# One load of 18 tile numbers per body, another order of PSUM banks, and a slot ring refilled in three parts, in a graph-network kernel of 49-tile passes

## The chip, the cores and the metric

The program runs on one core of one Trainium2 chip. The metric is the device time of one execution in microseconds (us), lower is better. A run of the program before takes 8250.26 us (median of 3).

## The reference

The work is a two-block graph transformer on 6250 nodes with 256 features and 100,000 edges sorted by destination. The part that the change touches is the sum over edges:

```python
def _rgcn_layer(X, W, root, bias, gamma, beta, src, dst, etype, inv_deg):
    h = jnp.einsum('ni,rio->rno', X, W)              # table of 4 x 6250 rows
    msg = h[etype, src] * inv_deg[:, None]
    agg = jax.ops.segment_sum(msg, dst, num_segments=X.shape[0])
    out = agg + X @ root + bias
    ...                                              # layer norm, elu, + X
for l in range(4): X = _rgcn_layer(X, ...)           # block 0
...
agg = segment_sum(all_h[src, rel], dst)              # block 1, once, 8 relations
```

Beside block 0 a linear-attention mixer on the same rows is computed (keys and values summed over all rows, then attention rows with a layer norm, then a feed-forward with a layer norm), beside block 1 the keys of a second mixer. Feed-forward stages follow both.

## The kernel before, in words

**Five passes over the edges.** The edges are cut into steps of 128 edges, and 17 steps (`SLOTS`) make a body; 49 bodies (`NT`) make a pass. There are four passes for block 0 (called passes 0 to 3 here) and one for block 1 (pass 4). In a body the engines do this, each in a hardware loop (`Fori`) of its own, joined by semaphores alone:

- POOL (`EdgeSum.gpsimd`, L530) issues one indirect DMA for each step, which gathers 128 message rows into slot s of `msg`.
- PE (`EdgeSum.tensor`, L579) multiplies the step's one-hot matrix `hot` (edge to row of the tile) by the messages into a PSUM bank.
- DVE (`EdgeSum.vector`, L559) adds the bank to the sum of the step's tile, whose number it reads from a register. It reads the numbers of the next 9 steps with `load_tiles` (L81, a register load from SBUF) ahead of step 0, and those of the other 8 ahead of step 9. A third load (`ranked_tile`, L88) of one word stands at the start of a body in passes 0 to 3.
- DVE makes 9 of the 17 one-hot matrices (L539), ACT the other 8 (`scalar_hots`: L508, L511, L520).
- ACT (`ring`, L497 and L498) copies the row numbers and edge data of the next body into a small ring, in two halves: steps 0 to 8 once PE has done them, then 9 to 16. POOL waits for that ring (`slots_copied`) before it gathers.

**Banks.** Step s uses bank 4 + s mod 4, so PE may be four steps ahead of DVE.

**What runs between the steps.** After step s each engine calls the hook `after(s)` of two other pieces. `Post` finishes one tile of the layer (norm, elu, new state: L624 to L649 on DVE after steps 0 to 8; transposes L672 and products L678, L684 on PE after steps 11 to 16; copies L694, L696, L701 on ACT), and SP stores the tile's two halves of the next table (L706). The mixer piece is `Keys0` in pass 0 (PE L785 and L791, ACT L801 to L803, DVE L811 and L814), `Attend` in pass 1 (PE L874 and L937, ACT L862, L950, L951, DVE L961) and `Feed` in pass 2 (PE L867, L874 and L1054, ACT L862, L1065, L1069). Pass 3 has only `Post` without the products, pass 4 only the keys of the second mixer. In these pieces the order on each engine is written out by hand; a wait blocks all that stands behind it on its engine.

## Time and profile before

| | |
|---|---|
| runs shown | 8244.22, 8250.26, 8263.54 us |
| profiled execution, its own time | 8245.88 us |
| its span in the trace | 8244.1 us |
| mean granted TensorE clock | 0.823 |
| busy: PE, DVE, POOL, ACT | 5874.8, 4269.0, 4208.5, 2931.9 us |
| passes 0, 1, 2 (first to last gather) | 571.9 to 1796.1, 1829.0 to 3072.8, 3108.4 to 4251.3 us |
| passes 3, 4 | 4280.0 to 5322.7, 6334.0 to 7373.9 us |

Busy times are sums of instruction durations on one engine, so they overlap. Idle time in a row (in square brackets) is that of the engine just before the instruction, with the one whose end released it; "issue" is idle time for which the profile shows no releaser. A matmul row with `x2` is one fp32 product in two passes.

### The profile page before, as it was taken

The numbers are of one execution on the slowest core, as the hardware profiler recorded it, in microseconds if no ns is written. First come the engines' busy times: TensorE is split into PE (matmuls) and PEld (weight loads), VectorE is DVE, ScalarE is ACT, GpSimd is POOL, SyncE is SP. The second block draws the span as 40 slices with busy tenths as digits, with TensorE's granted clock in tenths as the row PEclk, the third lists the DMA queues.
The fourth block names the chain that finished last, engine by engine and source line by source line (L and its number), as shares of the span: only waits on it lengthen the run. The fifth ranks groups of instructions, "written<-read, shape, count | busy, mean of one in ns | idle before, by whom it ended". The sixth has DMA issues, their size and how long they took to land. (4 is left out here: it accounts for less than half of the span.)

```text
span 8244.1 us, 110504 instructions
## 1 busy us (share of the span) xinstructions
PE 5874.8 (71%) x17886; PEld 3559.1 (43%) x17886; DVE 4269.0 (52%) x14582; ACT 2931.9 (36%) x8048; POOL 4208.5 (51%) x4288
## 2 busy tenths in 40 slices
PE   0487777767777776777768888788498777763398
PEld 0244444444444444554443333355344444443265
DVE  7215555546666665666656666522434666652412
ACT  0133333333444445666653333222022444431132
POOL 0016666656666656777667777600002777753211
PEclk9998888888888888889985556589599888877699
DMA  1444333334444434444443333300044333330000
GB/s 56 145 132 118 112 116 114 113 115 121 124 124 123 123 117 134 135 135 135 132 151 105 104 105 105 99 0 0 19 142 132 105 105 105 105 87 1 13 14 18
DMA packets 478956, 811.01 MB, mean 98 GB/s; under 512 B 88600, under 2 KB 343148, under 8 KB 478657
## 3 DMA queue, kind: packets, MB, share of 16 engines
q0 software_dynamic: 200480, 548.02, 23.2%
q1 hardware_dynamic: 278430, 262.51, 9.9%
q8 instruction: 13, 0.21, 0.0%
q14 instruction: 33, 0.27, 0.0%
HBM read 614.04 MB, written 196.16 MB: 98 GB/s over the span
## 5 line engine op out<-in xcount | busy, mean ns | idle before, releaser
L530 POOL DMA_INDIRECT gnn_msg<-tables,gnn_row_ring x4165 | 3985.8, 957 | 2183.9 <-issue 1585.2
L579 PE MATMUL bank<-gnn_msg,gnn_hot 128*128 128x256 f32 x8330 | 3143.3, 494 | 781.0 <-DVE sums L559 506.8
L559 DVE TENSOR_TENSOR sums<-sums,bank 128x256 f32 x4165 | 1746.0, 419 | 2060.0 <-PE bank L579 1360.7
L579 PEld LDWEIGHTS bank<-gnn_msg,gnn_hot 128*128 128x128 f32 x8330 | 1748.2, 237 | 2130.3 <-DVE sums L559 1424.8
L133 POOL TENSOR_TENSOR ve<-mv,eps 128x7 f32<-128x7 f32 x35 | 7.1, 204 | 1348.6 <-DVE mv L127 1200.3
L520 ACT ACTIVATE gnn_hot<-gnn_away,gnn_meta_ring 128x128 f32<-128x128 f32 x1568 | 645.8, 482 | 47.3 <-ACT gnn_meta_ring L511 0.8
L684 PE MATMUL bank<-gnn_w,residual 128*128 128x512 f32 x1176 | 620.1, 610 | 33.7 <-DVE sums L652 33.7
L508 ACT ACTIVATE gnn_away<-iota,gnn_meta_ring 128x128 f32<-128x128 f32 x1960 | 625.5, 391 | 24.0 <-ACT gnn_meta_ring L498 0.2
L539 DVE TENSOR_SCALAR gnn_hot<-iota,gnn_meta_ring 128x128 f32<-128x128 f32 x1764 | 629.1, 357 | 0.5 <-ACT gnn_meta_ring L498 0.5
L497 ACT COPY gnn_row_ring<-row 128x9 int32 (+1 forms) x490 | 94.9, 194 | 1070.3 <-PE bank L579 1058.5
L1760 PE MATMUL bank<-tables_w,sums 128*128 128x512 f32 x784 | 340.1, 596 | 6.4 <-ACTq L117 6.4
L701 ACT COPY residual<-bank 128x512 f32<-128x512 f32 x294 | 172.1, 585 | 284.0 <-PE bank L684 284.0
L684 PEld LDWEIGHTS bank<-gnn_w,residual 128*128 128x128 f32 x1176 | 219.9, 197 | 116.1 <-DVE sums L652 83.3
L658 ACT ACTIVATE gnn_own<-gnn_own 128x256 f32<-128x256 f32 x196 | 81.7, 417 | 442.2 <-DVE gnn_own L638 442.2
L1219 PE MATMUL bank<-gnn_w,gnn_hot 128*128 128x512 f32 (+1 forms) x588 | 221.0, 534 | 19.7 <-ACTq L1284 19.7
L1760 PEld LDWEIGHTS bank<-tables_w,sums 128*128 128x128 f32 x784 | 149.4, 191 | 193.2 <-issue 193.2
L678 PE MATMUL bank<-gnn_w,residual 128*128 128x256 f32 x588 | 222.3, 518 | 1.6 <-ACT residual L696 1.4
L874 PE MATMUL bank<-residual 128*128 128x128 f32 x784 | 155.5, 363 | 66.9 <-ACT residual L1065 64.5
L862 ACT ACTIVATE residual<-residual,gnn_own 128x256 f32<-128x256 f32 x98 | 58.8, 600 | 402.0 <-DVE residual L849 402.0
L696 ACT COPY residual<-bank 128x256 f32<-128x256 f32 x147 | 54.7, 372 | 395.3 <-PE bank L672 395.0
L874 PEld LDWEIGHTS bank<-residual 128*128 128x128 f32 x784 | 145.1, 269 | 107.2 <-ACT residual L1065 94.0
L1773 DVE COPY sums<-bank 128x512 f32<-128x512 f32 x98 | 67.7, 691 | 230.8 <-PE bank L1760 226.7
(390 smaller groups left out, 6866.1 us busy)
## 6 DMA issues: line engine op xcount, KB each, us to landing
tables<-residual SPq DMA_DIRECT2D x294, 256.0 KB
gnn_msg<-tables,gnn_row_ring POOLq DMA_INDIRECT x4165, 2.8
tables<-sums SPq DMA_DIRECT2D x98, 512.0 KB, 2.9
tables<-gnn_msg SPq DMA_DIRECT2D x98, 256.0 KB, 2.1
residual<-first_norm_columns SPq DMA_DIRECT2D x98, 128.0 KB, 2.4
first_norm<-state SPq DMA_DIRECT2D x1, 6272.0 KB, 21.4
first_rows<-residual SPq DMA_DIRECT2D x1, 6272.0 KB, 39.2
residual<-first_norm SPq DMA_DIRECT2D x49, 128.0 KB, 3.1
```

The lines of the kernel that those rows point to most:

```text
L508: self.nc.scalar.activation(self.away[:, k, :], self.c.iota[:], ACT.Abs, bias=m[:, u, 0:1], scale=-1.0)\
L520: ins = self.nc.scalar.activation(to, self.away[:, k, :], ACT.Relu, bias=m[:, u, 1:2], scale=m[:, u, 2:3])
L530: self.nc.gpsimd.indirect_dma_start(out=self.msg[:, s0 + u, :], out_offset=None, in_=table, in_offset=bass.IndirectOffsetOnAxis(ap=self.ro ...
L539: ins = self.nc.vector.tensor_scalar(to, self.c.iota[:], m[:, 0:1], m[:, 1:2], ALU.is_equal, ALU.mult)
L559: self.nc.vector.tensor_tensor(at, at, self.sums(s), ALU.add).then_inc(self.added, 1)
L579: self.nc.tensor.matmul(self.sums(s), self.hot[:, s, :], self.msg[:, s, :], start=True, stop=True).then_inc(self.summed, 1)
L678: ins = t.matmul(c.bank[1][:, 0:D], self.xt[:, h, :], self.w[:, h, REL0 * D:], start=(h == 0), stop=(h == KH - 1))
L684: ins = t.matmul(c.bank[3 - 2 * j][:], self.xt[:, h, :], self.w[:, h, j * 512:(j + 1) * 512], start=(h == 0), stop=(h == KH - 1))
L701: self.nc.scalar.copy(self.outs[:, j, :], self.c.bank[3 - 2 * j][:]).then_inc(self.s_out, 1)
L874: ins = self.nc.tensor.matmul(self.c.bank[0][:, m * P:(m + 1) * P], weights[:, h, m * P:(m + 1) * P], self.xt[:, h, :], start=(h == 0), st ...
L1219: ins = nc.tensor.matmul(c.bank[b][:, 0:width], xt[:, h, k * P:(k + 1) * P], w[:, h, j * 512:j * 512 + width], start=(h == 0), stop=(h == ...
L1760: ins = nc.tensor.matmul(c.bank[b][:], xt[:, h, k * P:(k + 1) * P], w[:, h, j * 512:(j + 1) * 512], start=(h == 0), stop=(h == KH - 1))
```

## The change

1. **Tile numbers.** `body_row` holds 18 words for each body: its 17 tile numbers and, behind them, the number of the tile that `Post` finishes. DVE loads all 18 once at the start of a body (`body_tiles`), in place of `load_tiles` twice and `ranked_tile` once. The row begins at the same SBUF address as before; a body's words now begin at word 18 i, where they began at words 17 i and 17 i + 9.
2. **Banks.** Steps 0 to 7 use banks 4 to 7 twice, steps 8 to 16 use banks 4, 5, 6 three times. Step 0 of a body follows step 14 on its bank, where it followed step 16.
3. **Three parts.** The ring is refilled in parts of 6, 6 and 5 steps. ACT makes 3 one-hot matrices in each (9 in all), DVE 3, 3 and 2 (8). On ACT part 0's refill moves ahead of the exponential, and part 0's one-hot matrices ahead of the copies of `Post.turned`.
4. **Mixer.** SP fetches the mixer rows of body i + 1 between the two table stores of body i, where it fetched them at the start of body i + 1. On PE the mixer's first products move from after step 5 to after step 3 (`Keys0`, `Attend`), in `Feed` from after steps 3, 6, 10 to after 2, 5, 9. On DVE `Attend`'s L961 moves from after step 9 to after step 6, and its L964 from 6 to 9.

```diff
-HALVES = ((0, 9), (9, 8))
+PARTS = ((0, 6), (6, 6), (12, 5))
-SUM_SLOTS = 4
+SUM_BANKS = (4, 5, 6, 7, 4, 5, 6, 7, 4, 5, 6, 4, 5, 6, 4, 5, 6)
...
-def load_tiles(eng, c, first, n):
-    regs = c.regs[str(eng.engine)][:n]
-    eng.reg_load(regs, c.tile_row[0:1, ds(first, n)])
+def body_tiles(eng, c, i):
+    regs = c.regs[str(eng.engine)]
+    eng.reg_load(regs, c.body_row[0:1, ds(i * (SLOTS + 1), SLOTS + 1)])
     return [eng.snap(r, min_val=0, max_val=NT - 1) for r in regs]
...
-DVE_HOTS = (5, 4)
-ACT_HOTS = 4
-NEXT_HOTS = (((), (), (0,), (), (1,), (), (2,), (), (3,)),
-             ((), (), (0,), (1,), (), (2,), (3,), (4,)))
+DVE_HOTS = (3, 3, 2)
+ACT_HOTS = 3
+NEXT_HOTS = (((), (), (0,), (), (1,), ()),
+             ((), (), (0,), (), (1,), (2,)),
+             ((), (), (0,), (1,), (2,)))
...
     def vector(self, dve, tiles, n, after, last=False):
-        for h, (s0, w) in enumerate(HALVES):
-            tiles = load_tiles(dve, self.c, i * SLOTS + s0, w)
-            for u, t in enumerate(tiles):
+        for h, (s0, w) in enumerate(PARTS):
+            for u in range(w):
                 s = s0 + u
+                t = tiles[s]
...
     def tensor(self, pe, n, after):
-            back = s - SUM_SLOTS + 1 if s >= SUM_SLOTS else max(k for k in range(SLOTS) if k % SUM_SLOTS == s) + 1 - SLOTS
-            pe.wait_ge(self.added, n * SLOTS + (SLOTS + back))
+            before = max(k for k in range(s - SLOTS, s) if SUM_BANKS[k] == SUM_BANKS[s])
+            pe.wait_ge(self.added, n * SLOTS + (SLOTS + before + 1))
...
 (SP, passes 0 to 2)
-                    with sp.Fori(1, NT) as i:
-                        work.sync(sp, i, True, True)
-                        post.sync(sp, i + l * NT, ranked_tile(sp, c, i - 1), c.tabs[(l + 1) % 2])
+                    with sp.Fori(1, NT - 1) as i:
+                        t = ranked_tile(sp, c, i - 1)
+                        work.store(sp, i, True, True)
+                        post.sync(sp, i + l * NT, t, c.tabs[(l + 1) % 2], 0)
+                        work.load(sp, i + 1)
+                        post.sync(sp, i + l * NT, t, c.tabs[(l + 1) % 2], 1)
...
 (ACT, passes 0 to 2)
                         work.scalar(act, i, True, True)
+                        edges.ring(act, i + 1, n + 1, 0)
                         post.exponential(act, n)
-                        edges.ring(act, i + 1, n + 1, 0)
+                        edges.scalar_hots(act, n + 1, 0)
                         post.turned(act, n, t)
-                        edges.scalar_hots(act, n + 1, 0)
+                        edges.ring(act, i + 1, n + 1, 1)
+                        edges.scalar_hots(act, n + 1, 1)
                         post.way_out(act, n, 0)
-                        edges.ring(act, i + 1, n + 1, 1)
+                        edges.ring(act, i + 1, n + 1, 2)
                         post.way_out(act, n, 1)
-                        edges.scalar_hots(act, n + 1, 1)
+                        edges.scalar_hots(act, n + 1, 2)
```

How this stands on the engines is shown at three places. Line numbers of the changed kernel are its own (L559 is L565 there, L520 is L525).

DVE at the start of the loop of pass 0, before: one word of `order` is loaded, then nine of `tile_row`, and then comes step 0's add.

```order
L1374 ISA
L88 TENSOR_LOAD order
L89 ISA
L81 TENSOR_LOAD tile_row
L82 ISA
L556 REGISTER_ALU
L557 REGISTER_ALU [waits steps_summed]
L559 ISA [waits steps_added]
L559 TENSOR_TENSOR sums<-sums,bank 128x256
```

Further down in the same body DVE had, between the last piece after step 8 and step 9's add:

```order
L649 SCALAR_TENSOR_TENSOR residual<-gnn_own,state 128x256
L81 ISA
L81 TENSOR_LOAD tile_row
L82 ISA
L559 ISA [waits steps_added,steps_summed]
L559 TENSOR_TENSOR sums<-sums,bank 128x256
```

The changed kernel has one load at the start, and none between steps 8 and 9:

```order
L1394 ISA
L81 TENSOR_LOAD body_row
L82 ISA x2
L562 REGISTER_ALU
L563 REGISTER_ALU [waits steps_summed]
L565 ISA [waits steps_added]
L565 TENSOR_TENSOR sums<-sums,bank 128x256
```

Three loads with 1 + 9 + 8 words have become one load with 18.

ACT in the body of pass 0, from the mixer's results to the copies of the new state, before (`post_turned` is signalled by PE's transposes L672):

```order
L803 COPY residual<-bank 128x2x128
L658 ACTIVATE gnn_own<-gnn_own 128x256 [waits gnn0_post_normal]
L661 ACTIVATE gnn_own<-gnn_own 128x256 [waits gnn0_post_negative_part]
L494 ISA
L497 ISA [waits steps_summed]
L497 COPY gnn_row_ring<-row 128x9
L498 ISA
L498 COPY gnn_meta_ring<-meta 128x9x2
L694 ISA [waits gnn0_post_state_made]
L694 COPY state<-residual 128x256
L696 COPY residual<-bank 128x256 [waits gnn0_post_turned]
```

The same stretch of the changed kernel:

```order
L503 COPY gnn_meta_ring<-meta 128x6x2
L664 ACTIVATE gnn_own<-gnn_own 128x256 [waits gnn0_post_normal]
L667 ACTIVATE gnn_own<-gnn_own 128x256 [waits gnn0_post_negative_part]
L509 ISA
L513 ACTIVATE gnn_away<-iota,gnn_meta_ring 128x128 [waits slots_copied]
L513 ACTIVATE gnn_away<-iota,gnn_meta_ring 128x128 x2
L516 ACTIVATE gnn_meta_ring<-gnn_meta_ring 128x6
L519 ISA
L525 ACTIVATE gnn_hot<-gnn_away,gnn_meta_ring 128x128 [waits distances_made]
L525 ACTIVATE gnn_hot<-gnn_away,gnn_meta_ring 128x128 x2
L700 ISA [waits gnn0_post_state_made]
L700 COPY state<-residual 128x256
```

The ring's copies now stand ahead of the two activations of the exponential, and seven activations for part 0's one-hot matrices stand between the exponential and the two copies.

SP in the loop of pass 0 in the changed kernel (L740 is the mixer's columns, L711 a table store):

```order
L711 ISA [waits gnn0_post_evicted]
L711 DMA tables_1<-residual 128x2x256
L739 REGISTER_ALU
L740 ISA [waits gnn0_keys_products]
L740 DMA residual<-first_norm_columns 128x256
L710 REGISTER_ALU
L711 ISA [waits gnn0_post_evicted]
L711 DMA tables_1<-residual 128x2x256
```

The columns stand between the two stores; before, they stood behind both and the loop's branch.

## Rows read from the trace of the kernel before

**Rows 1.** Windows, passes 0 to 4: length, busy PE, PEld, DVE, ACT, POOL, then PEclk.

```profile
700.00:1700.00 1000.00, 744.25 (x2203) 454.41 (x2203) 545.65 (x1868) 396.21 (x1221) 641.99 (x672) 0.84 0.39 114
1900.00:2900.00 1000.00, 729.41 (x2345) 470.02 (x2346) 618.80 (x2149) 401.07 (x1210) 642.25 (x666) 0.85 0.42 123
3200.00:4200.00 1000.00, 736.92 (x2640) 497.58 (x2640) 649.65 (x2260) 611.43 (x1494) 704.46 (x727) 0.89 0.46 135
4400.00:5200.00 800.00, 699.40 (x1277) 303.02 (x1276) 486.54 (x1649) 279.27 (x904) 605.54 (x638) 0.58 0.36 105
6500.00:7300.00 800.00, 569.05 (x1875) 360.81 (x1874) 493.74 (x2078) 329.02 (x1127) 604.96 (x641) 0.83 0.36 105
```

**Rows 2.** Waits in 700 to 1700 us (pass 0): total us, times, longest.

```profile
POOL gnn_msg L530 <- ACT gnn_meta_ring L498: 169.0, 69, 3.3
DVE sums L559 <- issue: 163.7, 70, 3.6
PEld bank L791 <- DVE residual L811: 162.2, 40, 4.5
```

**Rows 3.** Timeline of DVE, pass 0: adds of step 9, 0, 9, 0.

```profile
965.26 0.42 DVE L559 TENSOR_TENSOR sums<-sums,bank 128x256 f32 x1 [0.46 <-issue]
...
978.91 0.42 DVE L559 TENSOR_TENSOR sums<-sums,bank 128x256 f32 x1 [1.71 <-PE bank L579]
...
1016.55 0.42 DVE L559 TENSOR_TENSOR sums<-sums,bank 128x256 f32 x1 [1.69 <-issue]
...
1032.03 0.42 DVE L559 TENSOR_TENSOR sums<-sums,bank 128x256 f32 x1 [3.60 <-issue]
```

**Rows 4.** Timeline of DVE, step 0's adds: one in pass 3, two in pass 4.

```profile
4606.21 0.42 DVE L559 TENSOR_TENSOR sums<-sums,bank 128x256 f32 x1 [3.00 <-PE bank L579]
...
6511.34 0.42 DVE L559 TENSOR_TENSOR sums<-sums,bank 128x256 f32 x1 [1.19 <-PE bank L579]
...
6533.80 0.42 DVE L559 TENSOR_TENSOR sums<-sums,bank 128x256 f32 x1 [2.42 <-PE bank L579]
```

**Rows 5.** Timeline of PE in pass 0, and of ACT's one-hot matrices.

```profile
966.27 1.20 PE L791 MATMUL bank<-residual 128*128 128x129 f32 x4 [2.88 <-DVE residual L814]
...
1002.23 1.27 ACT L508 ACTIVATE gnn_away<-iota,gnn_meta_ring 128x128 f32<-128x128 f32 x4
...
1003.73 1.65 ACT L520 ACTIVATE gnn_hot<-gnn_away,gnn_meta_ring 128x128 f32<-128x128 f32 x4
```

**Rows 6.** Windows of 1 us in pass 0; PEclk is the third number from the end.

```profile
967.00:968.00 1.00, 1.00 (x5) 0.83 (x4) 0.00 (x0) 0.00 (x0) 0.83 (x1) 0.50 0.37 98
973.00:974.00 1.00, 1.00 (x5) 0.70 (x4) 0.25 (x1) 0.00 (x0) 0.70 (x2) 1.00 0.29 74
```

**Rows 7.** Timeline of one body of pass 1, from step 0's add.

```profile
2326.05 0.42 DVE L559 TENSOR_TENSOR sums<-sums,bank 128x256 f32 x1 [3.69 <-issue]
...
2333.93 0.42 ACT L661 ACTIVATE gnn_own<-gnn_own 128x256 f32<-128x256 f32 x1
...
2337.11 0.74 PE L937 MATMUL bank<-residual 128*128 128x132 f32 x4 [2.75 <-DVE residual L961]
...
2339.78 1.68 PE L678 MATMUL bank<-gnn_w,residual 128*128 128x256 f32 x4
```

**Rows 8.** Timeline of pass 2: end of a body, then the next body.

```profile
3604.36 0.30 PEld L684 LDWEIGHTS bank<-gnn_w,residual 128*128 128x128 f32 x2 [1.34 <-DVE sums L652]
...
3610.15 0.42 DVE L559 TENSOR_TENSOR sums<-sums,bank 128x256 f32 x1 [3.40 <-issue]
...
3611.83 0.66 PE L867 MATMUL bank<-ident,residual 128*128 128x128 f32 x2 [3.30 <-DMA residual<-mixer_rows]
...
3618.46 0.62 ACT L1069 ACTIVATE residual<-bank,residual 128x128 f32<-128x128 f32 x2 [0.86 <-PE bank L874]
...
3621.24 0.42 DVE L641 SCALAR_TENSOR_TENSOR gnn_own<-gnn_own 128x256 f32<-128x256 f32 x1 [1.39 <-ACT gnn_own L661]
...
3623.60 0.51 PEld L678 LDWEIGHTS bank<-gnn_w,residual 128*128 128x128 f32 x3 [0.35 <-ACT residual L696]
```

More of the change, by code:

```diff
@@ L779, in after @@
         def after(s):
-            if s == 5 and first:
+            if s == 3 and first:
                 pe.wait_ge(self.s_xt, i * 16 + 16)
@@ L927, in after @@
         def after(s):
-            if s == 5 and first:
+            if s == 3 and first:
                 pe.wait_ge(self.s_xt, i * 16 + 16)
@@ L1041, in after @@
         def after(s):
-            if s == 3 and first:
+            if s == 2 and first:
                 pe.wait_ge(self.s_dma, i * 16 + 16)
@@ L1973, in _ @@
                 gate(act, c)
-                for h in range(2):
+                for h in range(NPART):
                     edges.ring(act, 0, n0, h)
```

150 lines of the change are left out of this document (81 added, 69 removed).

## The prediction

> **What bounds the kernel now.** I read the windows over the five passes first. POOL issues 17 gathers for each body, so its count gives the time of a body: 17 x 1000 / 672 = 25.3 us in pass 0, 17 x 1000 / 666 = 25.5 in pass 1, 23.4 in pass 2, 21.3 in pass 3 and 21.2 in pass 4 [rows 1]. In passes 3 and 4 each gather follows the last after 800 / 640 = 1.25 us. POOL never rests there, so 21.25 us is the floor of a body as long as there are 17 gathers in it, and passes 3 and 4 stand on it. Passes 0 to 2 lie 4.1, 4.3 and 2.1 us above it. The change does not touch the gathers, so it can win (4.1 + 4.3 + 2.1) x 47 = 490 us at most. (I count 47 full bodies in a pass of 49; the first and last run without their neighbours.)
>
> In pass 0 POOL waits for the ring 69 times in 1000 us, 169 us together, but in that list no PE wait for a message stands among the long ones. POOL's waits follow from something else. The list names it: DVE stands idle 163.7 us in 70 waits for nothing the profile knows ("issue"), and PE's L791 waits 162.2 us in 40 bodies for DVE [rows 2]. The reader should see that PE and DVE take turns. At the start of a body PE runs its four steps ahead and then needs DVE's step 0; in the middle L791 needs DVE's L814 after step 9; from there to step 16 DVE follows PE. A stall of DVE ahead of step 0 or step 9 is therefore paid in full.
>
> Both stalls are register loads. Ahead of step 9 DVE is idle 1.69 us, or 0.46 in every fourth body; ahead of step 0 it is idle 3.60, or 1.71 in every fourth [rows 3]. The fast ones are the bodies in which the load begins at a word number that is a multiple of four (17 i or 17 i + 9); the other three remainders are alike. Four bodies hold 3 x 1.69 + 0.46 and 3 x 3.60 + 1.71, which is 1.38 + 3.13 = 4.5 us of stall a body.
>
> **The change, part by part.**
>
> *The loads.* I estimate a price for one word. Eight words cost 1.69 - 0.46 = 1.23 us more when they begin off a multiple of four, and nine words 2.42 - 1.19 = 1.23 in pass 4 [rows 3, 4]. If an unaligned load goes word by word and an aligned one by groups of four with single words left over, that is 8 against 2 reads and 9 against 3: six more both times, 0.205 us each, and 8 x 0.205 = 1.64 is the whole unaligned gap. The one-word load is the difference of pass 3 and pass 4, which has none: 3.00 - 2.42 = 0.58 [rows 4]. What is left at the start of a body is 1.19 - 3 x 0.205 = 0.57 for branch and rest. In pass 0 the unaligned start has 0.6 us more than in pass 3 (3.60 against 3.00); SP and ACT load words then too, so I keep it as a collision.
>
> Now 18 words begin at 18 i: a multiple of four in even bodies only. Even: 4 groups and 2 words, 0.57 + 6 x 0.205 = 1.8 us. Odd: 18 reads, 0.57 + 3.69 + 0.6 = 4.9 us. Mean 3.35, and nothing before step 9. Bounds: if 18 words cost 1.8 always, 1.8; if they never go by fours, 0.57 + 18 x 0.205 = 4.3; if the collision also grows with the words, 5.5. I take the middle, since both kinds of body are seen.
>
> The Trainium skill speaks against this part: "Runtime: NRT & Kernel Launch", Instruction fetch mechanics, gives about 200 ns for each register even in bulk. The unaligned rows agree with it, the aligned ones do not. By that rule 18 words before and 18 after cost the same 3.6 us, and only the fixed parts of two loads would be saved.
>
> *Pass 0.* Without its loads a body is 25.3 - 4.5 = 20.8 us. Added: 3.35, which gives 24.15. L785 moves ahead of step 4, into the time in which PE waits for DVE; that PE idle shrinks and costs nothing elsewhere. Its columns are fetched between the stores, which is sooner by one store and the branch. DVE makes one one-hot fewer by step 9 (-0.3), but with none after step 6 it meets the exponential 0.3 sooner and waits for it. ACT now makes three one-hots before the new state's copies: 1.27 + 1.65 for four plus 0.2 for the scaling is 3.15, so 2.42 for three [rows 5]. In pass 0 L672 comes only after L791, and ACT is free by then: hidden, with about 1.4 us to spare; without that cover it would add 1. One more term is PE's clock. After 2.88 us of idle PE starts L791 [rows 5], and the granted clock is 0.50 (1.2 GHz) at 967 us and 1.00 (2.4 GHz) again at 973 [rows 6]. PE's idle falls to about 2.3 us. Whether the clock still drops I can't tell from a row; full recovery would save about 2 us a body, none saves 0. I take 0.7, as the 2.88 of the nearest row still led to a drop. Body: 23.4, a gain of 1.9.
>
> *Pass 1.* The same stalls are there [rows 7]: 25.5 - 4.5 + 3.35 = 24.35. Here L937 waits 2.75 us for L961, which stood after step 9 and now stands after step 6. PE goes on until it needs the new state. ACT sets the next point: L661 ends 8.3 us after step 0's add (2326.05 to 2334.35), the one-hots take 2.42, the two copies 0.8, so L678 starts at 11.6 where it started at 13.7, 0.5 of which is the aligned load already counted. That is 1.6 earlier. PE's idle is now cut in small pieces, for which I take 0.6 of clock. Body: 22.2, a gain of 3.3.
>
> *Pass 2.* Here the middle load hides: DVE waits 1.39 for L661 before step 8 anyway, and PE waits 1.34 for L652 later on [rows 8]. ACT is the path: the norm, the copy, L1069 (which waits 0.86 for PE's L874), the exponential, then L694 and L696, then L678. The ring's copies ahead of the exponential add 0.3, the one-hots add 2.42 less the 1.4 that ACT idled there. On the other side PE no longer waits 3.30 for the mixer rows, so its clock should stay up in L874, which gives back the 0.86. From step 0's add (3610.15) L678 started at 13.45; now 11.1 + 0.3 - 0.86 + 2.42 + 0.8 = 13.75. That is 0.3 late. L684 waited 1.34 for L652, which now comes sooner; I count 0.7 of it, since DVE has its own instructions to do between step 9 and L652. The start costs 3.35 instead of some 3.0 (3.40 in the row, less the aligned quarter). The body is 23.4 + 0.3 - 0.7 + 0.35 = 23.3, a gain of 0.1; if none of the 1.34 comes back it is 24.0, if all does 22.7.
>
> *Passes 3 and 4.* The start of an odd body grows from 3.0 to about 4.3, but the load in the middle is gone, and POOL is the bound. POOL needs PE's step 16 only 12 gathers (15 us) after its own. Cost and gain nothing. The third ring wait, the new banks (step 11 now needs step 8's add instead of step 7's, in a stretch in which DVE waits for PE) and the two small copies in the preparation are hidden or below 1 us.
>
> *Sum.* (1.9 + 3.3 + 0.1) x 47 = 249 us. The profiled execution took 8245.9, which gives 7997. The median of the runs is 4 us higher; I say 7998.
>
> **Rivals.**
>
> (a) The clock recovers and the load is as I think: pass 0 goes to 22.1, pass 1 to its floor 21.3, pass 2 to 22.8. Another 2.7 x 47 = 127 us: 7870. For it: PE will be idle for less time at a stretch than ahead of the row in which the clock had fallen; against it, by little. Chance 0.15.
>
> (b) The load of 18 is cheap in all bodies (1.8): 21.85, 21.3 and 21.75, a gain of 9.3 x 47 = 437: 7809. For it speaks only that 8 and 9 words pay the same penalty, which a fixed penalty would explain too. Chance 0.12.
>
> (c) The load never goes by fours, 4.3 a body: 24.35, 23.15, 24.25, a gain of (0.95 + 2.35 - 0.85) x 47 = 115: 8131. This is the rule of the skill named above as a mechanism of this kernel; the aligned rows speak against it. Chance 0.13.
>
> (d) As (c), and ACT's new order eats what the clock and L961 would give: 25.0, 25.2, 24.1, together zero: about 8246. Chance 0.05.
>
> (e) Slower: the load costs 5.5 in every body, because a longer load meets SP's and ACT's own loads more often. The place is the start of the bodies of passes 0 to 2, where 4.5 is paid now. With pass 1 held at 21.0 + 5.5 it gives 25.6, 26.5 and 25.4, or (0.3 + 1.0 + 2.0) x 47 = 155 us more: 8401. It decides from about 4.9 us a load, if pass 1 gains nothing else. Only the 0.6 of collision speaks for it. Chance 0.08.
>
> **How the numbers follow.** My forecast has 0.47. The range 7860 to 8135 holds it with (a) and (c) and leaves out (b) and (e); the forecast's own range is 7930 to 8060. A measurement of this kernel can tell about 0.2% (16 us) from no change. Faster: 0.47 + 0.15 + 0.12 + 0.13 = 0.87; same 0.05; slower 0.08.
>
> **What the profile after would show.** No DVE idle before step 9; before step 0 an idle that alternates between about 1.8 and 4.9 us. Gathers per 1000 us: 726 in pass 0, 766 in pass 1, 730 in pass 2, and 1.25 us apart in passes 3 and 4 as before. In pass 1 L937 without a wait for DVE and L678 some 11.6 us after step 0's add; in pass 2 ACT's L696 late. I am wrong if the start of a body costs much more or less than 3.35 on average, if PE's clock behaves otherwise, or if passes 3 or 4 leave the floor.

## The result and the profile after

The changed kernel takes 8075.3 us (median of 4 runs, 8071.81 to 8077.64), the kernel before 8256.88 us in the runs beside it (4 runs, 8244.22 to 8263.54). The ratio is 0.9779, 95% interval 0.9765 to 0.9794. It is faster by 182 us where the prediction said 249, and 8075 lies 15 us outside the forecast's own range of 7930 to 8060, inside the wide one of 7860 to 8135. The profiled execution took 8071.81 us, its span is 8070.0 us, and its mean granted clock 0.81 (before 0.823).

Windows over passes 0 to 3 after the change (length, busy PE, PEld, DVE, ACT, POOL, PEclk):

```profile
700.00:1700.00 1000.00, 788.92 (x2337) 459.37 (x2338) 564.23 (x1927) 468.03 (x1499) 675.16 (x709) 0.85 0.41 120
1850.00:2850.00 1000.00, 820.63 (x2740) 508.30 (x2740) 711.01 (x2478) 517.02 (x1652) 741.77 (x770) 0.86 0.49 143
3050.00:4050.00 1000.00, 729.27 (x2511) 492.88 (x2512) 622.12 (x2104) 622.00 (x1623) 663.37 (x686) 0.84 0.43 127
4250.00:5050.00 800.00, 678.85 (x1273) 290.63 (x1272) 477.70 (x1614) 321.41 (x1082) 606.13 (x637) 0.61 0.36 104
```

Against [rows 1], pass 0 goes from 672 to 709 gathers (726 forecast), pass 1 from 666 to 770 (766 forecast), and pass 2 falls from 727 to 686 (730 forecast). Pass 2 has become slower. Pass 3 stays at its floor with 637 against 638.

Step 0's adds on DVE after the change, two in pass 0 and two in pass 4; the bracket is DVE's idle time before them:

```profile
1055.45 0.42 DVE L565 TENSOR_TENSOR sums<-sums,bank 128x256 f32 x1 [2.24 <-PE bank L585]
...
1081.17 0.42 DVE L565 TENSOR_TENSOR sums<-sums,bank 128x256 f32 x1 [5.25 <-issue]
...
6591.41 0.42 DVE L565 TENSOR_TENSOR sums<-sums,bank 128x256 f32 x1 [2.29 <-PE bank L585]
...
6613.44 0.42 DVE L565 TENSOR_TENSOR sums<-sums,bank 128x256 f32 x1 [4.64 <-issue]
```

The idle alternates as forecast, but both kinds are dearer: 2.24 and 5.25 us in place of 1.8 and 4.9. Their mean of 3.75 us stands against the 4.5 that two stalls a body cost before [rows 3]. In passes 0 to 2 no idle time is left ahead of step 9.

One body of pass 1, from step 0's add (the counterpart of [rows 7]):

```profile
2217.35 0.42 DVE L565 TENSOR_TENSOR sums<-sums,bank 128x256 f32 x1 [2.30 <-PE bank L585]
...
2226.22 1.09 PE L946 MATMUL bank<-residual 128*128 128x132 f32 x4
...
2228.75 1.13 PE L684 MATMUL bank<-gnn_w,residual 128*128 128x256 f32 x4
```

L946 (L937 before) had waited 2.75 us for DVE and now waits for nothing. L684 (L678 before) starts 11.4 us after step 0's add; 11.6 was forecast.

One body of pass 2 (the counterpart of [rows 8]):

```profile
3316.85 0.42 DVE L565 TENSOR_TENSOR sums<-sums,bank 128x256 f32 x1 [2.26 <-issue]
...
3316.94 0.41 PE L874 MATMUL bank<-ident,residual 128*128 128x128 f32 x2 [1.20 <-DMA residual<-mixer_rows]
...
3322.89 0.35 ACT L1075 COPY residual<-bank 128x256 f32<-128x256 f32 x1
...
3323.29 2.03 PE L881 MATMUL bank<-residual 128*128 128x128 f32 x8 [4.08 <-ACT residual L1075]
...
3325.36 0.62 ACT L1079 ACTIVATE residual<-bank,residual 128x128 f32<-128x128 f32 x2 [0.82 <-PE bank L881]
...
3326.32 0.42 DVE L565 TENSOR_TENSOR sums<-sums,bank 128x256 f32 x1 [2.05 <-PE bank L585]
...
3327.89 0.42 ACT L667 ACTIVATE gnn_own<-gnn_own 128x256 f32<-128x256 f32 x1
...
3330.57 0.39 ACT L700 COPY state<-residual 128x256 f32 x1
3330.86 0.36 ACT L702 COPY residual<-bank 128x256 f32<-128x256 f32 x1
...
3331.28 0.92 PE L684 MATMUL bank<-gnn_w,residual 128*128 128x256 f32 x3 [0.43 <-ACT residual L702]
```

Ahead of the transposes L874 (L867 before) PE waits 1.20 us for the mixer rows in place of 3.30, but in the next place, right ahead of L881 (L874 before), it waits 4.08 us for ACT in place of 1.30. L881 then takes 2.03 us at the lower clock, the Gelu L1079 still waits 0.82 us for it, DVE waits 2.05 us ahead of step 6 because the edge steps stand behind L881 on PE, and L684 starts 14.4 us after step 0's add instead of 13.5.

### The profile page after: what moved, and what is told of

Its sections match the earlier page's. It is cut to its first block and busy times, and to the rows that moved or that the text cites. A ratio compares the mean times of both kernels' runs of the same rounds, so it can differ in the third digit from the quotient of the medians.

```text
span 8070.0 us, 113767 instructions
## 1 busy us (share of the span) xinstructions
PE 5892.5 (73%) x17886; PEld 3531.1 (44%) x17886; DVE 4224.8 (52%) x14339; ACT 3200.3 (40%) x9224; POOL 4209.5 (52%) x4288
## 3 DMA queue, kind: packets, MB, share of 16 engines
q0 software_dynamic: 200480, 548.02, 23.7%
## 5 line engine op out<-in xcount | busy, mean ns | idle before, releaser
L585 PE MATMUL bank<-gnn_msg,gnn_hot 128*128 128x256 f32 x8330 | 3234.9, 506 | 852.2 <-DVE sums L565 625.6
L565 DVE TENSOR_TENSOR sums<-sums,bank 128x256 f32 x4165 | 1744.6, 419 | 1958.0 <-PE bank L585 1166.2
L585 PEld LDWEIGHTS bank<-gnn_msg,gnn_hot 128*128 128x128 f32 x8330 | 1771.3, 240 | 2266.1 <-DVE sums L565 1523.3
L525 ACT ACTIVATE gnn_hot<-gnn_away,gnn_meta_ring 128x128 f32<-128x128 f32 x1764 | 742.5, 483 | 70.0
L513 ACT ACTIVATE gnn_away<-iota,gnn_meta_ring 128x128 f32<-128x128 f32 x2205 | 721.8, 390 | 52.9
L544 DVE TENSOR_SCALAR gnn_hot<-iota,gnn_meta_ring 128x128 f32<-128x128 f32 x1568 | 555.1, 354 | 3.3 <-ACT gnn_meta_ring L503 3.3
L502 ACT COPY gnn_row_ring<-row 128x6 int32 (+1 forms) x735 | 143.1, 195 | 888.2 <-PE bank L585 875.7
L881 PE MATMUL bank<-residual 128*128 128x128 f32 x784 | 153.5, 357 | 206.5 <-ACT residual L1075 176.5
L881 PEld LDWEIGHTS bank<-residual 128*128 128x128 f32 x784 | 132.6, 255 | 248.8 <-ACT residual L1075 203.7
L684 PE MATMUL bank<-gnn_w,residual 128*128 128x256 f32 x588 | 188.3, 449 | 25.5 <-ACT residual L702 24.3
L1501 PE MATMUL bank<-sums,ffn_w 128*128 128x512 f32 (+1 forms) x448 | 175.6, 554 | 4.8 <-ACTq L117 4.8
```

Source lines behind the costliest of these rows:

```text
L513: self.nc.scalar.activation(self.away[:, k, :], self.c.iota[:], ACT.Abs, bias=m[:, u, 0:1], scale=-1.0)\
L525: ins = self.nc.scalar.activation(to, self.away[:, k, :], ACT.Relu, bias=m[:, u, 1:2], scale=m[:, u, 2:3])
L544: ins = self.nc.vector.tensor_scalar(to, self.c.iota[:], m[:, 0:1], m[:, 1:2], ALU.is_equal, ALU.mult)
L565: self.nc.vector.tensor_tensor(at, at, self.sums(s), ALU.add).then_inc(self.added, 1)
L585: self.nc.tensor.matmul(self.sums(s), self.hot[:, s, :], self.msg[:, s, :], start=True, stop=True).then_inc(self.summed, 1)
L684: ins = t.matmul(c.bank[1][:, 0:D], self.xt[:, h, :], self.w[:, h, REL0 * D:], start=(h == 0), stop=(h == KH - 1))
```

## The experiments

All bodies below are in us. They are the time from the first to the last gather of a pass over 832 / 17 = 48.94 bodies, read in the trace of one execution of each kernel. Kernels that share a pass's code agree in it to about 0.2 us in passes 0 to 2, so smaller differences say nothing. e4 scatters more than the others: its four runs took 8088 to 8135 us, and 46 us would be 0.9 us in each body of one pass. Its trace is from a run of 8130. "Ratio" is against the kernel before, run beside each on the same chip (medians 8256.88 us for the change, 8269.03 for e1 to e4, 8258.10 for e5 to e8, 8257.29 for e9 to e12). Offsets from step 0's add are means over bodies 3 to 48 of a pass; a pass's first and last body are shorter, so such a mean of the whole body is 0.1 to 0.3 us above the table's.

| kernel | pass 0 | 1 | 2 | 3 | 4 | median us | ratio, 95% interval |
|---|---|---|---|---|---|---|---|
| before | 25.01 | 25.41 | 23.35 | 21.31 | 21.25 | 8256.88 | |
| after | 23.71 | 21.83 | 24.48 | 21.39 | 21.30 | 8075.3 | 0.9779, 0.9765 to 0.9794 |
| e1_pad20 | 22.91 | 21.57 | 23.04 | 21.31 | 21.25 | 7949.98 | 0.9617, 0.9601 to 0.9633 |
| e2_shift1 | 24.04 | 23.28 | 25.93 | 21.31 | 22.37 | 8293.18 | 1.0031, 1.0020 to 1.0043 |
| e3_feed_hooks | 23.52 | 21.81 | 24.43 | 21.33 | 21.25 | 8071.99 | 0.9765, 0.9749 to 0.9782 |
| e4_load_only | 22.91 | 24.69 | 23.71 | 21.38 | 21.30 | 8126.77 | 0.9815, 0.9786 to 0.9844 |
| e5_by_pass | 22.95 | 23.87 | 25.14 | 21.39 | 21.30 | 8158.94 | 0.9875, 0.9855 to 0.9895 |
| e6_by_pass | 21.36 | 21.71 | 24.12 | 21.33 | 21.26 | 7922.24 | 0.9596, 0.9579 to 0.9613 |
| e7_banks_back | 23.69 | 21.83 | 24.49 | 21.37 | 21.30 | 8063.74 | 0.9766, 0.9750 to 0.9782 |
| e8_sp_back | 23.71 | 22.03 | 24.42 | 21.34 | 21.27 | 8074.69 | 0.9779, 0.9763 to 0.9795 |
| e9_pad_best | 21.33 | 21.58 | 23.11 | 21.32 | 21.25 | 7851.15 | 0.9502, 0.9486 to 0.9518 |
| e10_exp_first | 21.33 | 21.56 | 23.29 | 21.30 | 21.25 | 7862.99 | 0.9521, 0.9505 to 0.9537 |
| e11_words20 | 21.37 | 21.52 | 22.77 | 21.46 | 21.26 | 7845.49 | 0.9499, 0.9483 to 0.9515 |
| e12_mixer_back | 21.39 | 23.41 | 24.30 | 21.34 | 21.25 | 8021.40 | 0.9715, 0.9699 to 0.9731 |

### What the load costs: e1_pad20, e2_shift1, e11_words20

The rows of `body_row` become 20 words long. In e1 each load of 18 words then begins at a multiple of four, in e2 one word behind it.

```diff
-    eng.reg_load(regs, c.body_row[0:1, ds(i * (SLOTS + 1), SLOTS + 1)])
+    eng.reg_load(regs, c.body_row[0:1, ds(i * STRIDE + OFF, SLOTS + 1)])   # STRIDE 20; OFF 0 in e1, 1 in e2
```

> The changed kernel with 20 words for each body instead of 18 (two unused), so that every load of 18 words begins at a multiple of four. Theory W (a load that begins off a multiple of four is read word by word): DVE's idle before step 0 is 2.2 to 2.3 us in every body, the 5.2 us disappears; passes 0 and 2 gain half of 3.0, 1.5 us a body, pass 1 gains 0.6 down to the gather floor of 21.3, passes 3 and 4 nothing: (1.5 + 0.6 + 1.5) x 47 = 170, about 7905 us against the 8075 of the changed kernel. Rival R (every register costs the same wherever its word lies): the alternation stays or turns into 3.7 everywhere, about 8075.

> As the run with 20 words a body, but the whole row shifted by one word, so that no load begins at a multiple of four. Theory W: 5.2 us of idle before step 0 in every body of passes 0 to 2, 4.6 in passes 3 and 4; passes 0 and 2 grow by 1.5 us a body, pass 1 by 1.5 too, passes 3 and 4 stay near the floor: about 8075 + 210 = 8285, slower than the kernel before. A rule by pairs of words (a start at an even word is cheaper) is excluded already if 5.2 is seen here as for starts at even words. Rival R: as the changed kernel, 8075.

Step 0's add in pass 0 and in pass 4, in e1:

```profile
1064.60 0.42 DVE L566 TENSOR_TENSOR sums<-sums,bank 128x256 f32 x1 [2.24 <-PE bank L586]
...
6481.07 0.42 DVE L566 TENSOR_TENSOR sums<-sums,bank 128x256 f32 x1 [2.16 <-PE bank L586]
```

and in e2:

```profile
1092.82 0.42 DVE L566 TENSOR_TENSOR sums<-sums,bank 128x256 f32 x1 [5.22 <-issue]
...
6799.96 0.42 DVE L566 TENSOR_TENSOR sums<-sums,bank 128x256 f32 x1 [4.65 <-issue]
```

The idle time no longer alternates: it is the cheap one in every body of e1 and the dear one in every body of e2. One word of offset is worth 343 us (7949.98 against 8293.18), and nothing else differs in the program. In pass 4 an aligned load of 18 saves 4.65 - 2.16 = 2.49 us, which is 12 reads of 0.207 us. The prediction had 12 reads of 0.205 from the loads of 8 and 9 words. In passes 0 to 2 the difference is 3.0 us, so the 0.6 us that an unaligned load costs there besides (5.22 against 4.65) is real too, and it does not grow with the words: it was 0.6 with nine [rows 3, 4]. In e2 the load is so long that pass 4 leaves the floor (22.37).

What the load costs the body is another question. Between e1 and e2 the start grows by the same 3.0 us in passes 0 to 2, but pass 0 grows by 1.13 us only (22.91, 23.71, 24.04), pass 1 by 1.71 (21.57, 21.83, 23.28) and pass 2 by 2.89. e1 was expected to gain 1.5 us in pass 0 and gained 0.80. In pass 1 e1 comes close to POOL's floor. In pass 0 it is PE's clock: L684 (L685 in e1 and e2) takes less than 1.2 us in 9 of 46 bodies in e1, in 21 in the changed kernel and in 40 in e2 (1.75, 1.53 and 1.23 us on average), and step 16's add comes 20.28, 19.58 and 18.45 us after step 0's. So there 1.8 of the 3.0 us of a shorter start are lost again to slower steps. Why the clock follows the start in this way was not looked for.

e11 is e9 (below) with 20 words in place of 18, the last two unused, so that a load is five whole groups of four.

```diff
+    eng.reg_load(regs, c.body_row[0:1, ds(i * STRIDE, STRIDE)])
```

> The kernel e9_pad_best with 20 words read in place of 18 (the last two are copies and unused), so that a load is five groups of four and no single words. The starts seen so far in pass 4 are 1.19 us for 9 words and 2.16 for 18 when they begin at a multiple of four, 2.42 and 4.65 when not. Theory G (a single word costs 0.248, a group of four 0.361, the rest 0.22; that fits all four): 20 words need 0.22 + 5 x 0.361 = 2.03, 0.13 less than 18 words. Rival of the prediction (a group costs as much as a word, 0.205, and each register has a fixed price besides of 0.03 to 0.05): 18 words are 6 reads, 20 are 5 but with two registers more, 2.16 - 0.205 + 0.1 = 2.05, so hardly told apart. Rival L (the time goes with the number of words, and alignment gives a fixed discount): 2.16 + 2 x 0.108 = 2.38. Time within 10 us of e9_pad_best, by G 5 to 15 us less, by L 10 to 25 us more.

Step 0's add in pass 0 and in pass 4:

```profile
1030.63 0.42 DVE L570 TENSOR_TENSOR sums<-sums,bank 128x256 f32 x1 [2.01 <-issue]
...
6365.00 0.42 DVE L570 TENSOR_TENSOR sums<-sums,bank 128x256 f32 x1 [1.93 <-PE bank L590]
```

Reading two more words made each load 0.23 us shorter. Rival L, by which the time goes with the number of words, falls. So does theory G's pair of prices, which gave 0.13. What fits is the price of the prediction, one read of about 0.205 us for a word or a group of four: five reads against six. What did not carry over is the rest. In pass 4 it is 1.19 - 3 x 0.205 = 0.57 us for nine words, but 2.16 - 6 x 0.205 = 0.93 for 18 and 1.93 - 5 x 0.205 = 0.91 for 20. Why a load of 18 has 0.35 us more of it than one of 9 is open; it isn't a price for each register, or 20 words would show it. The time of e11 can't be told from e9's (7839.94 to 7848.69 against 7834.67 to 7860.42).

### The load alone: e4_load_only

The kernel before with one load of 18 words, rows of 18 as in the change, and nothing else.

```diff
-            tiles = load_tiles(dve, self.c, i * SLOTS + s0, w)
-            for u, t in enumerate(tiles):
+            for u in range(w):
                 s = s0 + u
+                t = tiles[s]
...
```

> The kernel before with the single load of 18 words alone (halves, banks, hooks, SP as before). Measured starts of 2.24 and 5.24, mean 3.74, in place of 3.13 + 1.38: pass 0 25.3 - 0.8 = 24.5, pass 1 25.5 - 0.8 = 24.7, pass 2, where the middle load is hidden, 23.4 + 0.75 = 24.1: (0.8 + 0.8 - 0.7) x 47 = 42 us less than before, about 8213. Rival (the load is the whole gain): about 8075. Rival (fewer words off the path do nothing because PE's clock eats them): 8255.

About 8213 us was expected; it took 8127, so the load alone brings 142 us, where the whole change brings 182. With runs from 8088 to 8135 the shares by pass that follow are less sure than those of the other kernels. It gained 2.10 and 0.72 us a body in passes 0 and 1 and lost 0.36 in pass 2. The stalls alone account for 4.5 - 3.75 = 0.75 a body. In pass 0 there is 1.35 us more, and it is PE's clock: with no stall ahead of step 9 PE waits 2.24 us on average ahead of L795 (L791 before), where it waited 3.68 on average (the 2.88 of [rows 5] is one of the short ones). In two of three bodies read in windows of 1 us the granted clock stayed at 1.00 behind that wait, and the product L684 (L678 before, L682 in e4) takes less than 1.2 us in 34 of 46 bodies, before in 13. Seen against e4, the rest of the change costs pass 0 0.8 us, wins 2.9 in pass 1 and costs 0.8 in pass 2. The next experiments take it apart.

### One edit for each pass: e5_by_pass

```diff
 (Keys0, PE: L792)
-            if s == 3 and first:
+            if s == 5 and first:
 (Attend, DVE: L970, and L973 from 9 to 6)
-            if s == 6 and first:
+            if s == 9 and first:
 (ACT, pass 2 only)
-                        edges.scalar_hots(act, n + 1, 0)
                         post.turned(act, n, t)
+                        edges.scalar_hots(act, n + 1, 0)
```

> The changed kernel with one edit in each of the first three passes, whose bodies don't touch each other, so each pass is read by itself (body of the changed kernel: 23.7, 21.8, 24.5 us in passes 0, 1, 2). Pass 0: Keys0's first products go back from after step 3 to after step 5. Theory C (they kept PE busy just ahead of its long wait for DVE after step 9; gone from there, the clock is low when PE comes back, and steps 10 to 13 take 0.9 us longer): body 22.8 to 23.0. Rival S (the ring in three parts or ACT's order costs pass 0 its 0.8 us): stays at 23.7. Pass 1: on DVE the et addition goes back from after step 6 to after step 9, and the gamma product from 9 to 6, while PE's first products stay after step 3. Theory D (the addition's place is the whole gain of this pass, 2.9 us over the kernel with the load alone): body 24.5 to 24.9. Rival P (it needs both, and PE's move is part of the gain): 23 to 24. Pass 2: the copies of the new state go ahead of part 0's one-hot matrices on ACT. Theory A (ACT's queue sets the end of this chain: PE's products after step 12 start 0.87 us later than with the load alone, of which 0.27 is the slower product L881, 0.18 the ring's copies, and the rest the one-hot matrices): body 24.1. Rival B (nothing in ACT's order matters, PE's clock does): 24.5. Sum for C, D, A: 8075 - 42 + 140 - 20 = about 8153. Sum for S, P, B: about 8155 as well, so the passes decide and not the total.

Pass 0 returned to 22.95, the value with the load alone, so the 0.8 us were L792's move. L792 had filled PE's time between steps 5 and 9. Windows of 1 us of the changed kernel, where its L684 stands and, in the next body, 5.8 and 12.8 us after step 0's add (PEclk is the third number from the end):

```profile
1068.00:1069.00 1.00, 1.00 (x3) 0.60 (x3) 0.41 (x3) 0.88 (x5) 0.73 (x1) 0.50 0.43 131
1087.00:1088.00 1.00, 1.00 (x3) 0.52 (x3) 1.00 (x4) 0.00 (x0) 0.69 (x2) 0.50 0.26 70
1094.00:1095.00 1.00, 1.00 (x5) 0.65 (x5) 0.59 (x3) 0.72 (x4) 0.00 (x0) 0.77 0.00 0
```

and of e5 where its L684 stands:

```profile
1055.00:1056.00 1.00, 0.97 (x5) 0.54 (x5) 0.97 (x3) 0.75 (x4) 0.75 (x1) 1.00 0.30 78
1056.00:1057.00 1.00, 1.00 (x7) 0.87 (x6) 0.10 (x1) 0.91 (x4) 0.69 (x2) 1.00 0.27 82
```

In the changed kernel PE is at 1.2 GHz in the stretch after step 9 in which DVE follows it (L684 takes 1.91 us there), in e5 at 2.4 GHz (1.13 us). Not every body is so: L684 takes less than 1.2 us in 21 of 46 bodies of the changed kernel and in 33 of e5 (1.53 and 1.36 us on average). L792 still costs nothing in its new place, as the prediction said. What was lost is the work that stood ahead of PE's long wait. That its place slows the clock is shown; in what way is not.

Pass 1 came to 23.87, in the range of rival P: the place of L970 is worth 2.0 us of the gain, not all 2.9. Pass 2 contradicts theory A. With the copies first, L684 started 14.22 us after step 0's add on average, against 14.33. ACT was free sooner, but PE reached the transposes L678 only at 13.38 (13.17 in the changed kernel). The body even grew by 0.66, which neither theory foresaw, and its start by 0.8:

```profile
3463.36 0.42 DVE L565 TENSOR_TENSOR sums<-sums,bank 128x256 f32 x1 [6.00 <-PE bank L585]
...
3487.47 0.42 DVE L565 TENSOR_TENSOR sums<-sums,bank 128x256 f32 x1 [2.75 <-issue]
```

Measured from the end of DVE's last instruction to step 0's add, the start is 3.0 and 6.1 us on average in place of 2.24 and 5.27. ACT's way-outs are later and SP issues a store, the mixer rows and the second store within 1.6 us just then; that this slows the load is a guess.

### The other way round: e6_by_pass

```diff
 (Keys0, DVE: L818, L821)
-            if s == 9 and first:
+            if s == 6 and first:
 (Attend, PE: L881)
-            if s == 3 and first:
+            if s == 5 and first:
 (Feed, ACT)
-        if second:
-            self.norm(act, i)
         if first:
             ...
             sc.copy(self.xt.rearrange("p h r -> p (h r)"), c.bank[0][:, 0:D]).then_inc(self.s_xt, 1)
+        if second:
+            self.norm(act, i)
```

> The changed kernel with another edit in each of the first three passes. Pass 0: on DVE Keys0's addition and column copy go from after step 9 to after step 6, as Attend's did. Theory (PE then no longer waits 1.95 us ahead of L798, which is what the change did for pass 1): body 21.8 to 22.0, and the clock stays up in steps 10 to 13. Rival (without the wait ahead of L798 PE waits as long for the new state ahead of its transposes): 23.3 or more. Pass 1: PE's first products go back from after step 3 to after step 5, DVE's addition stays after step 6. Theory (DVE then waits after step 6 for PE and ACT by about 0.8 us, paid once): body 22.5. Rival (PE's move was worth nothing): 21.8. Pass 2: ACT copies the turned rows first and norms afterwards, so L881 no longer waits for the norm. Theory (the chain norm, copy, L881, Gelu loses L881, and the Gelu comes 0.8 us earlier, right behind its table load): body 23.7. Rival (the chain through DVE's norm input is as long without L881, or L881 now lies in front of the edge steps and delays them): 24.3 to 24.6. Sum: 8075 - 90 + 35 - 40 = about 7980; by the rivals about 8055.

Windows over passes 0, 1 and 2:

```profile
700.00:1500.00 800.00, 674.58 (x2101) 389.43 (x2100) 493.27 (x1710) 418.20 (x1349) 605.98 (x637) 0.91 0.46 135
1750.00:2650.00 900.00, 703.88 (x2479) 447.10 (x2478) 639.25 (x2232) 465.76 (x1493) 676.46 (x705) 0.91 0.49 144
2850.00:3850.00 1000.00, 765.00 (x2542) 469.37 (x2542) 622.10 (x2134) 633.47 (x1644) 678.29 (x698) 0.89 0.44 129
```

Pass 0 reaches 637 gathers in 800 us: it stands on POOL's floor like passes 3 and 4, and DVE's pieces moved by three steps were worth 2.35 us a body, more than the 1.7 to 1.9 expected. Pass 1 shows no loss with L881 after step 5, so PE's part of the move was worth nothing there. In pass 2 the chain moved as meant but the time didn't follow:

```profile
3262.14 1.28 ACT L667 ACT_TABLE_LOAD   x1
3263.44 0.42 ACT L667 ACTIVATE gnn_own<-gnn_own 128x256 f32<-128x256 f32 x1
...
3263.89 0.43 DVE L647 SCALAR_TENSOR_TENSOR gnn_own<-gnn_own 128x256 f32<-128x256 f32 x1 [1.99 <-ACT gnn_own L667]
...
3266.83 2.07 PE L684 MATMUL bank<-gnn_w,residual 128*128 128x256 f32 x4 [0.43 <-ACT residual L702]
```

The exponential L667 came 1.1 us earlier (9.84 after step 0's add on average, 10.92 in the changed kernel), and so did L684 (13.25 against 14.33). But the clock now falls behind the new wait ahead of the elu L647, and L684 takes 1.56 us on average instead of 1.11 (2.07 in this row). Step 16 is only 0.34 us earlier. The body of 24.12 lies between the theory (23.7) and the rival (24.3 to 24.6). The rival's loss is there, but it came from the clock and not from L881's new place.

### Parts that cost nothing: e3_feed_hooks, e7_banks_back, e8_sp_back

e3 puts Feed's three products on PE back after steps 3, 6 and 10; e7 restores the old banks; e8 puts SP's fetch of the mixer rows back to the start of the loop.

```diff
 (e7)
-SUM_BANKS = (4, 5, 6, 7, 4, 5, 6, 7, 4, 5, 6, 4, 5, 6, 4, 5, 6)
+SUM_BANKS = tuple(4 + s % 4 for s in range(17))
 (e8, SP's loop, the new lines alone)
...
+                        work.load(sp, i)
                         work.store(sp, i, True, True)
+                        t = ranked_tile(sp, c, i - 1)
+                        for j in range(2):
+                            post.sync(sp, i + l * NT, t, c.tabs[(l + 1) % 2], j)
```

> The changed kernel with the feed-forward's products in pass 2 put back to after steps 3, 6 and 10 on PE. Theory H (PE sits blocked by L881 after step 5 while ACT waits for the norm, its clock falls and step 6 is late for DVE): DVE's wait of 2.05 us at step 6 goes, PE's idle before L881 falls from 4.1 us, pass 2 goes from 24.7 to 23.2 to 24.0 us a body: 8075 - 35 to - 70. Rival A (ACT's chain alone, the ring's copies and the one-hots, sets pass 2): no change beyond 15 us.

> The changed kernel with the old bank order (4 + s mod 4), so that step 0 of a body again follows step 16 on its bank. Theory (DVE's load of 3.7 us at the start of a body covers PE's steps 0 to 3 either way): bodies within 0.1 us of the changed kernel's in all passes, time 8075 within 15. Rival (the order was worth something: PE gets one step further ahead): 0.3 to 0.4 us a body in passes 0 to 2, 8120 to 8135.

> The changed kernel with SP's fetch of the mixer rows back at the start of the loop. Theory (their place was worth something only where PE waits for them: with the products now after step 3 instead of 5 the late rows would be waited for in passes 0 and 1, since L792 waited 0.44 and L881 0.5 to 1.1 us for them even with the early fetch; and pass 2's turn waits for rows but lies ahead of a longer wait): pass 0 by +0.3 to +1.0, pass 1 by +0.3 to +1.0, pass 2 within 0.2. Time 8105 to 8175. Rival (PE's waits for the rows lie inside its wait for DVE at the start of a body, whose load covers 3.7 us): all passes within 0.1, 8075.

Each of them leaves every body within 0.2 us of the changed kernel's. In e3 DVE's wait of 2.05 us moved from ahead of step 6 to ahead of step 7, where it is 1.4 us, and L684 stayed at 14.31 after step 0's add, so where Feed's products stand does not matter by itself. In e8 the fetch comes late enough that PE waits for it again (3.5 us ahead of L874 in pass 2), and the time is the same: either wait lies ahead of the longer one for L1075. In passes 0 and 1 the late fetch costs one step, ahead of step 4 (DVE's step 4 comes 0.4 and 0.3 us later); pass 0 gives it back later in the body, and pass 1 shows 0.2 us.

### The mixer part undone: e12_mixer_back

SP as in e8, Feed as in e3, Attend wholly as before (PE after 5, DVE after 9 and 6), Keys0's products after step 5 but its DVE pieces after step 6.

```diff
 (Attend: PE, then DVE)
-            if s == 3 and first:
+            if s == 5 and first:
...
-            if s == 6 and first:
+            if s == 9 and first:
```

> The changed kernel with nearly all of the mixer part undone: SP's fetch of the rows back at the start of the loop, Feed's products back after steps 3, 6, 10, Attend's wholly as before (PE 5, DVE 9 and 6), Keys0's products back after step 5, but Keys0's DVE pieces after step 6. Pass 2: theory M (the fetch and the places on PE together, not each by itself, made PE idle 3.7 us in one piece ahead of L881 where it was idle 1.3, and so slowed the clock): L881 takes 1.7 in place of 2.0 and the body is 24.0 to 24.1. Rival (the three parts and ACT's order cost it): 24.4. Pass 1: theory (the mixer part is the whole 2.9 us over the kernel with the load alone): 24.5 to 24.8; rival (three parts, banks and ACT's order are worth something too): 23.9, as with the DVE part undone alone. Pass 0: theory (with the DVE pieces after step 6 the place of the products on PE no longer matters): 21.3 to 21.6; rival (products after step 5 hold DVE's piece up): 21.9 to 22.3.

Pass 0 (21.39) shows that L792's place matters only as long as PE has the long wait after step 9. Pass 1 (23.41) is below both forecasts (23.9 and 24.5). It divides the 2.9 us: 1.6 are the mixer part, and 1.3 (24.69 to 23.41) belong to the ring's parts and ACT's order, since the banks did nothing in e7. The two were not tried apart, and the shares don't add up: with L970's place undone alone 2.0 were lost (e5), with the whole mixer part 1.6, so with L970 after step 9 the rest of the mixer part costs 0.5. Pass 2 is not settled by it: L881 took 1.82 us on average, between the 1.71 of the load alone and the changed kernel's 1.99, and the body's 24.30 lies within the scatter of 24.48.

### Towards a better kernel: e9_pad_best, e10_exp_first

e9 joins e1's rows of 20 words, e6's DVE pieces in Keys0 and e6's order of copy and norm in Feed. e10 also puts the exponential ahead of the Gelu in pass 2, and Feed's last products on PE after step 11 in place of 9:

```diff
 (Feed, PE)
-            if s == 9 and first:
+            if s == 11 and first:
 (ACT, pass 2 only; the Gelu stood ahead of these lines)
-                        edges.ring(act, i + 1, n + 1, 0)
                         post.exponential(act, n)
-                        edges.scalar_hots(act, n + 1, 0)
+                        edges.ring(act, i + 1, n + 1, 0)
+                        work.gelu(act, i)
                         post.turned(act, n, t)
+                        edges.scalar_hots(act, n + 1, 0)
```

> The changed kernel with rows of 20 words (18 read, each load at a multiple of four), Keys0's DVE pieces after step 6 and Feed's copy ahead of the norm. Theory (the parts add up, down to the floor of 21.25 us a body that POOL's gathers set): the pad alone took 0.8, 0.26 and 1.44 us a body in passes 0 to 2, the other two edits 2.35 in pass 0 and 0.36 in pass 2. Pass 0 is at its floor (21.3), pass 1 at 21.5, pass 2 at 22.7: 8075 - 49 x (2.4 + 0.3 + 1.8) = 7855. Rival (a shorter start only moves the wait: in pass 2 the clock falls later in the body, as it did when the copy went ahead of the norm, where 0.7 of the 1.1 us won on ACT was lost again): pass 2 stays at 23.0 to 23.3, time 7875 to 7885.

> The kernel e9_pad_best with another order on ACT in pass 2 (norm, exponential, ring, Gelu, the copies of the new state, then part 0's one-hot matrices), and Feed's last products on PE after step 11 in place of 9. Theory (DVE's wait of 2.0 us ahead of the elu, for the exponential that stands behind the Gelu and its table load, is the largest wait left in the pass): the elu comes 1.4 us earlier, pass 2 falls by 1.0 to 1.4 us to about 21.6: 55 us less than e9_pad_best. Rival Q (the Gelu and Feed's last products are late in its place, and DVE waits for them ahead of step 12's piece): no gain, within 0.3 us of it. Rival R (the one-hot matrices and way-outs behind the copies delay the stores, and the start of a body costs 0.9 us more, as in e5_by_pass): pass 2 slower by 0.5.

e9 takes 7851 us, 5.0% less than the kernel before and 224 us less than the change. Four of the five passes are at or within 0.4 us of the floor of 21.25. Pass 2 stayed at 23.11, as its rival said. In e10 DVE's wait ahead of the elu fell from 2.0 to 1.4 us, but step 12's add then came 1.95 us after step 11's, where it had come 0.74 after it, because Feed's last products now stand there: rival Q, no gain. The two waits of pass 2 are exchanged for each other.

## Why the prediction was right, and where it was off

The sign, the alternating start, the free middle and the two passes at the floor were as forecast. In the trace's bodies the change won 1.30 + 3.58 - 1.13 - 0.08 - 0.05 = 3.62 us over the five passes, times 48.94 bodies 177 us; the two profiled executions differ by 174. The prediction had 1.9 + 3.3 + 0.1. Pass 2 alone is 1.23 us a body, 58 us, short of it, and pass 0 another 0.6, of which pass 1 gives back 0.28.

Three terms were read from a single body that was not a typical one. L791's wait was 2.88 us in [rows 5] and 3.68 on average; L678 began 13.7 us after step 0's add in [rows 7] and 15.0 on average; L1069's wait for L874 was 0.86 in [rows 8] and 0.38 on average. That the total comes out as near as it does is in part luck.

**The loads.** The mechanism was right: groups of four, 0.205 us a read, 0.6 more for an unaligned load in passes 0 to 2 (e1, e2, e11). Mis-sized was "0.57 for branch and rest", taken from a load of nine words: with 18 it is 0.93. The start costs 3.75 us on average, not 3.35, in each of three passes. Paid in full that would be 0.4 x 3 x 47 = 56 us. But that a stall ahead of step 0 "is therefore paid in full" is wrong for pass 0: 1.5 us more of start cost 0.80, 0.26 and 1.44 us a body in passes 0, 1 and 2 between e1 and the change. At these prices 0.4 us are an estimated 0.2 + 0.1 + 0.4 a body, some 30 us. That the loads alternate speaks against the rivals (b), (c) and (e), which had one price for all bodies. By the rule of the Trainium skill ("Runtime: NRT & Kernel Launch", Instruction fetch mechanics: about 200 ns for each register even in bulk) 18 words would take 3.6 us wherever they begin, as an estimate from that figure. e2 agrees with it (12 reads more cost 2.49 us), e1 does not, where the whole idle time is 2.16 us.

**Pass 0** (1.9 forecast, 1.30 measured). Counted as stalls, 0.4 of the gap is the load (0.75 in place of 1.15 saved). The 0.7 for the clock was nearly right as a sum (1.30 - 0.75 = 0.55) by luck, for it was wrong in its parts: the load alone gave back 1.35, and L785's move (L792 now), of which the prediction said that it "costs nothing elsewhere", took 0.8 (e4, e5).

**Pass 1** (3.3 forecast, 3.58 measured). The dearer load was made up for: beyond it there are 2.83 us, against 2.15 in the forecast. The place of L970 was worth 2.0 of them (e5). L684 started at 11.4 (11.5 on average) where 11.6 was said, but from 15.0 on average and not from 13.7, so it came 3.5 us sooner and not 2.1.

**Pass 2** (0.1 forecast, -1.13 measured) failed, and the step is "its clock should stay up in L874, which gives back the 0.86". Means over the bodies of the pass, in us from step 0's add:

| | before | e4, load alone | after |
|---|---|---|---|
| L881 (L874) starts | 6.26 | 6.36 | 6.35 |
| it takes | 1.54 | 1.71 | 1.99 |
| L667 (L661) ends | 10.62 | 10.90 | 11.34 |
| L678 (L672) starts | 12.18 | 12.62 | 13.17 |
| L684 (L678) starts | 13.07 | 13.46 | 14.33 |
| step 16's add | 19.77 | 19.42 | 20.28 |
| next step 0's add | 23.43 | 23.90 | 24.73 |
| bodies of 46 in which L881 takes under 1.4 us | 23 | 17 | 0 |

L881 waits for ACT's norm and copy, which no part of the change moves, so what PE no longer waited for the rows became a longer wait right ahead of L881. The clock during L881, in the body shown above:

```profile
3324.00:3325.00 1.00, 1.00 (x7) 1.00 (x6) 0.28 (x1) 0.54 (x1) 0.89 (x1) 0.50 0.40 115
```

It did not stay up: L881 took 0.45 us longer than before, where the forecast took 0.86 off. No more than 0.38 could be had there on average, since in half of the bodies before L874 already ran at the higher clock (1.2 us). L684 starts 1.26 later on average. The term for L684's old wait for L652 (-0.7) held: from L684 to step 16 it is now 5.95 us, before 6.70. The rest is 0.79 at the end of the body and the start, 0.35 in the forecast. The 1.26 go down two paths of almost the same length. One is the chain on ACT that the prediction added up: L667 ends 0.72 later (0.45 for L881, 0.18 for the ring's copies ahead of the exponential, 0.09 for L881's start), the one-hot matrices take 2.26 and the copies 0.73, without idle time on ACT, and 11.34 + 2.26 + 0.73 = 14.33. The other is PE, which reaches the transposes L678 1.0 late. e5 took the matrices out of the first and gained only 0.1 by it, since L678 then held L684 up.

Which part of the change lowered the clock is open in part. The load alone left 17 of the 23 fast bodies. Of the rest, the products' places (e3, 1 fast body), the banks (e7, none), the fetch (e8, 4) and the one-hot matrices' place (e5, none) each leave it nearly so when undone alone; the places and the fetch undone together (e12) bring back 11. The three parts and the ring's copies were not tried alone.

**Passes 3 and 4** stayed within 0.1 us of the floor, as forecast; e2 shows that it takes 4.65 us in every body of pass 4 to leave it.

## What to carry to other kernels

Let a register load from SBUF begin at a multiple of four words and fill up the last group: here rows of 20 words in place of 18 were worth 125 us (7949.98 against 8075.3; 134 by the two ratios), and reading two unused words made a load shorter, though the total time didn't show it. When a wait is removed, look for the wait that lies behind it on the same engine before counting a gain, and count what the work that is moved did where it stood: on PE, work ahead of a long wait held the clock for the stretch after it. Take a fixed remainder from a row of the same size, not from one half as large, and take a term from the mean over many bodies: where the clock has two levels, a single body shows one of two cases.
